# One change to a perceiver block: transposed inputs, and a first cross attention that goes by pairs of tiles

## The chip, the core and the metric

The kernel runs on one core of a Trainium2 chip. TensorE is called PE here, VectorE DVE, ScalarE ACT, GpSimd POOL, SyncE SP; SPq and ACTq are the DMA issues of SP and ACT. The metric is the device time of one execution in microseconds, and the median of the runs is what counts.

## The reference, cut to what matters

`x` is 32 x 64 x 128 (the latents), `ctx_1024` is 32 x 1601 x 128 (the context), both f32. Six layers follow one another, each added to `x`:

```python
x = x + L0_xattn(layernorm(x), ctx, ctx, mask, Wq, bq, Wk, bk, Wv, bv, Wo, bo)  # 16 heads of 8
x = x + L0_attn(layernorm(x), ...)           # a delta rule by chunks of 64
x = x + L0_ffn(layernorm(x), router, up, dn) # 8 experts, top 2
x = x + L1_xattn(ctx, layernorm(x), Wq, Wkv, Wout, gm, bm, gl, bl)
x = x + L1_attn(layernorm(x), ...)           # a gated delta rule, 4 heads
x = x + L1_ffn(layernorm(x), ...)            # attention over the batch, then 8 experts
# in L0_xattn, per batch and head:
#   softmax(q @ k.T * scale, masked keys out) @ v, then @ Wo.T + bo
# in L1_xattn (8 heads of 64): keys and values from concat(ln(ctx, gm, bm), ln(latents, gl, bl)) @ Wkv,
#   queries from ln(latents, gl, bl) @ Wq; softmax of q @ k.T / scale minus its maximum
```

`scale` is the head size to the power -1/2, so in L1_xattn the division by it makes scores large: both cross attentions need the row maximum before the exponential, and precise scores.

## The kernel before, in words

The stages run one after another: setup and **xattn0** (0 to 1098 us), **delta0**, **moe0**, **xattn1** (1426 to 2562 us), **delta1**, **ffn1** (from 2846 us). Each stage writes one instruction list per engine; semaphores alone order the engines, and each list is in a fixed, hand-written order. The latents stay on chip in `k.x` (16 tiles of 128 rows).

**xattn0** (`stage_xattn0`) takes one step per batch, 32 steps; steps 0 and 27 to 31 are written out, the others are in a loop of two. The 1601 keys are 13 tiles of 128 (the last has 65). What a step `b` does:

- *Scores* (`scores`, L794): for tile `j`, eight bf16 products of the stacked keys `KS` with the queries `QS` of all 16 heads, into the two-bank tensor `SC`. The keys are split in three bf16 pieces `KP[0..2]`, whose stack of 97 rows plus bias rows is multiplied in one go. ACT takes the exponential into `PT` (`probs`, L522).
- *Products* (`products`, L805, L809): `PT` times the values `V` in f32, 8 instructions. The row sums come from POOL's running sum `acc` (L444) of nine tiles, closed by `total` (L817), and for the other tiles from a product with ones (L809).
- *Maxima* for the next batch (`tops`, L771, L775): 26 units, each a bf16 product of the keys with the queries into one of the two banks `A`, and a reduction on DVE (L607, L610). `top` (L784) transposes the result `mxm` into `M`, and `topped` (L621, DVE) writes it as the rows of `QS` that subtract the maximum.
- *Context and keys* for later batches: four transposes `turn(b+3)` (L732) into the bank `M`, copied by ACT (`turned`, L486) to `CT`; `keys(b+2, c)` (L743) and `values(b+2, c)` (L759) for the four column chunks; then `keys` on ACT (first piece, L494), `residue` on DVE (L590), `second` on ACT, `third` on POOL (L433).
- *Transfers*, all on SP: `load(b+4)`, then two `spill`s of `KP` to memory (`KD`, L353; 12 issues), then two `stack`s of eight transfers each back into `KS` (L363), with the bias rows (L359).

At the front, the query weights are transposed, the layer norm of `x` and the queries are made, split into three pieces, written to memory (`QD`) and spread by heads into `QP` (L333, `spread`): batches 0 to 7 from SP, the others from ACT. The order there on SP is spill 0 (two halves), the pieces, stack 0 first half, spread, stack 0 second half, then batch 1.

**xattn1** (`stage_xattn1`) also has one step per batch, with 8 pairs of tiles `u`. The context is loaded again by rows into `C`, and its layer norm is made three batches ahead: `stats` and `moments` (DVE), `power` (POOL, L1639), `norm` (DVE, L1869, 13 tensor_scalar). `turn`/`turned` transposes it; `gain` (POOL, L1646, L1656) makes the value side. The maxima of the next batch are `tops` (L2036 on PE, L1875 on DVE), closed by `top` (L1884, L2047, L1888). At its start the stage loads ten weight tensors and transposes three (L1977), makes the products `GH` and `HH` (L1986, L1988), and only then transposes the norm (L220).

**Layer norm of the latents** (`norm_vector`, `norm_pool`, `norm_tensor`, `norm_scalar`): DVE takes 16 statistics (L188), 16 aggregates (L191), one addition (L194 or L196), POOL one power of 16 columns (L208), DVE 16 scalings (L201), PE 16 transposes (L220) in four chunks, ACT four copies. **ffn1** starts with four weight transposes (L2841 to L2844) ahead of them, and with two DVE copies that regroup weights (L2753, L2764).

The step of xattn0 on PE, which the change rewrites:

```python
for j in range(NK):
    us = units(j) if n1 else ()
    for u in us[0:1]: tops(b + 1, 1 - a, u)
    if j + 1 < NK: scores(b, a, j + 1)
    elif n1: scores(b + 1, 1 - a, 0)
    for u in us[1:2]: tops(b + 1, 1 - a, u)
    ...                       # keys, values, turn
    for u in us[2:]: tops(b + 1, 1 - a, u)
    products(b, a, j)
```

## Time and profile before

| | us |
|---|---|
| median of 3 runs | 3082.73 (3077.76 to 3084.12) |
| the profiled execution | 3079.37 |
| its span, and mean granted clock | 3077.6, 0.962 |
| PE busy | 2819.4 (92%), weight loads 1618.6 (53%) |
| DVE busy | 1978.6 (64%) |
| ACT busy | 1479.6 (48%) |
| POOL busy | 1906.0 (62%) |
| DMA | 233.18 MB, mean 76 GB/s |
| POOL sums L444 | 596.7 in 252 instructions of 2368 ns |
| ACT exponentials L522 | 425.8 in 416 |
| DVE maxima L607 | 506.4 in 768 of 685 ns |

Busy shares are means over stages of different make: PE is near 95% in both cross attentions and 60 to 80% at the stage starts. A timeline row gives start, duration, engine, line and operands, and in brackets the idle time before it with what ended it; a matmul row's end is modelled, so starts of neighbours are the safer measure.

### The profile page before, as it was taken

To read this page: it belongs to the slowest core of one execution; us is meant where nothing else is said; L and a number is where in the kernel's file an instruction comes from. 1 tells how busy PE (TensorE), PEld (TensorE's weight loads), DVE (VectorE), ACT (ScalarE), POOL (GpSimd) and SP (SyncE) were. 2 spreads that over 40 slices of the span, in tenths; PEclk is the share of its full clock that TensorE was granted. 3 is DMA by queue.
4 is the path that set the end of the run, shared out by engine and by line. 5 is a ranking of instruction groups with operands and counts; after the bars stand their busy time and mean duration, and the time that the engine had idled before them with its cause. 6 is when DMAs were issued, how large, how long until landed. Compare 5 with 4: busy or idle time off the path is not lost. (4 is left out here: it accounts for less than half of the span.)

```text
span 3077.6 us, 66754 instructions
## 1 busy us (share of the span) xinstructions
PE 2819.4 (92%) x22718; PEld 1618.6 (53%) x22765; DVE 1978.6 (64%) x4504; ACT 1479.6 (48%) x2385; POOL 1906.0 (62%) x1278
## 2 busy tenths in 40 slices
PE   5799999999999978998899999999999997888789
PEld 2355555555555566775344444444444443777356
DVE  5477777777777744114667767767767744776653
ACT  3466666666666522333544444444444434223633
POOL 5487878787878721001488888888888872553500
PEclk8899999999999989998999999999999998999789
DMA  7655555555555210001000000000000000000300
GB/s 184 187 174 193 177 190 181 184 186 179 194 175 188 100 58 1 1 0 39 22 33 21 21 32 21 21 32 21 21 32 21 21 1 9 3 3 2 85 5 10
DMA packets 146463, 233.18 MB, mean 76 GB/s; under 512 B 16787, under 2 KB 85851, under 8 KB 146076
## 3 DMA queue, kind: packets, MB, share of 16 engines
q1 hardware_dynamic: 145180, 228.87, 22.7%
q10 hardware_dynamic: 1152, 2.49, 0.6%
q8 instruction: 91, 1.49, 0.2%
q14 instruction: 40, 0.33, 0.0%
HBM read 147.80 MB, written 83.52 MB: 75 GB/s over the span
## 5 line engine op out<-in xcount | busy, mean ns | idle before, releaser
L444 POOL TENSOR_TENSOR sb_a_acc<-sb_a_acc,sb_a_PT 128x1024 f32<-128x1024 f32 x252 | 596.7, 2368 | 36.6 <-ACT sb_a_PT L522 30.3
L522 ACT ACTIVATE sb_a_PT<-ps_a_SC 128x1024 f32<-128x1024 f32 (+1 forms) x416 | 425.8, 1023 | 315.3 <-PE ps_a_SC L794 291.7
L607 DVE TENSOR_REDUCE sb_a_mx<-ps_a_A 128x1 f32<-128x512 f32 x768 | 506.4, 685 | 97.0 <-PE ps_a_A L771 91.8
L1686 POOL TENSOR_TENSOR sb_a_acc<-sb_a_acc,sb_a_PT 128x512 f32<-128x512 f32 (+2 forms) x384 | 487.5, 1269 | 37.3 <-ACT sb_a_PT L1782 10.9
L1782 ACT ACTIVATE sb_a_PT<-ps_a_SC 128x1024 f32<-128x1024 f32 (+2 forms) x256 | 234.3, 915 | 563.0 <-PE ps_a_SC L2061 329.3
L1875 DVE TENSOR_REDUCE sb_a_mx<-ps_a_A 128x1 f32<-128x512 f32 x384 | 256.5, 679 | 280.1 <-PE ps_a_A L2036 240.1
L2080 PE MATMUL ps_a_PV<-sb_a_PT,sb_a_XN 128*128 128x512 f32 (+2 forms) x896 | 434.3, 601 | 2.2 <-ACT sb_a_PT L1782 0.7
L2061 PE MATMUL ps_a_SC<-sb_a_QX,sb_a_XT 128*128 128x512 f32 (+1 forms) x832 | 396.7, 596 | 0.1
L771 PE MATMUL ps_a_A<-sb_a_KS,sb_a_QS 97*128 97x512 bf16 x768 | 301.9, 394 | 30.6 <-issue 17.7
L794 PE MATMUL ps_a_SC<-sb_a_QS,sb_a_KS 105*128 105x128 bf16 (+1 forms) x3328 | 257.3, 220 | 13.4 <-DVE sb_a_QS L621 13.4
L805 PE MATMUL ps_a_PV<-sb_a_PT,sb_a_V 128*32 128x256 f32 (+1 forms) x3328 | 266.7, 392 | 0.4 <-issue 0.3
L794 PEld LDWEIGHTS ps_a_SC<-sb_a_QS,sb_a_KS 105*128 105x128 bf16 (+1 forms) x3328 | 217.8, 99 | 83.8 <-ACT sb_a_PT L522 23.2
L2061 PEld LDWEIGHTS ps_a_SC<-sb_a_QX,sb_a_XT 128*128 128x128 f32 (+1 forms) x832 | 152.0, 186 | 202.3 <-issue 199.7
L2080 PEld LDWEIGHTS ps_a_PV<-sb_a_PT,sb_a_XN 128*128 128x128 f32 (+2 forms) x896 | 163.5, 191 | 131.3 <-issue 117.2
L208 POOL TENSOR_TENSOR sb_rstd<-sb_rstd,sb_half 128x16 f32<-128x16 f32 x8 | 23.3, 2907 | 291.9 <-DVE sb_rstd L194 240.9
L444 POOL TENSOR_TENSOR sb_a_acc<-sb_a_PT 128x1024 f32<-128x1024 f32 x32 | 75.4, 2357 | 199.7 <-ACT sb_a_PT L522 199.7
L1646 POOL TENSOR_TENSOR sb_a_XN<-sb_a_C,sb_a_gm 128x1536 f32<-128x1536 f32 x64 | 123.6, 1956 | 92.8 <-PE ps_a_PV L2080 92.1
L771 PEld LDWEIGHTS ps_a_A<-sb_a_KS,sb_a_QS 97*128 97x128 bf16 x768 | 74.5, 97 | 181.9 <-DVE sb_a_mx L607 106.2
L1869 DVE TENSOR_SCALAR sb_a_C<-sb_a_C,sb_a_cag,sb_a_crs 128x128 f32<-128x128 f32 (+1 forms) x416 | 170.0, 480 | 0.0
L1453 DVE SCALAR_TENSOR_TENSOR sb_x<-ps_a_D,sb_a_comb,sb_x 128x128 f32 x128 | 36.2, 344 | 180.7 <-PE ps_a_D L1407 180.5
L1431 ACT ACTIVATE sb_a_H<-ps_a_U 128x512 f32<-128x512 f32 x128 | 76.2, 597 | 139.4 <-PE ps_a_U L1398 139.3
L1656 POOL TENSOR_TENSOR sb_a_XN<-sb_a_XN,sb_a_bm 128x1536 f32<-128x1536 f32 x64 | 122.9, 1940 | 30.9 <-PE ps_a_PV L2017 23.1
(516 smaller groups left out, 5265.3 us busy)
## 6 DMA issues: line engine op xcount, KB each, us to landing
sb_a_C<-in_ctx_dram SPq DMA_DIRECT2D x64, 768.0 KB
a_KD<-sb_a_K SPq DMA_DIRECT2D x192, 256.0 KB, 4.1
sb_a_KS<-a_KD SPq DMA_DIRECT2D x256, 192.0 KB
a_KD<-sb_a_K SPq DMA_DIRECT2D x192, 144.2 KB, 2.7
sb_a_KS<-a_KD SPq DMA_DIRECT2D x256, 108.2 KB
sb_a_QP<-a_QD ACTq DMA_DIRECT2D x6, 384.0 KB, 14.7
sb_a_up<-in_moe_up_dram SPq DMA_DIRECT2D x1, 2048.0 KB, 7.9
sb_a_dn<-in_moe_dn_dram SPq DMA_DIRECT2D x1, 2048.0 KB, 12.0
```

Source lines behind the costliest of these rows:

```text
L444: pool.tensor_tensor(acc[:, :], first[:, :], PT[slot(a, j)][:, :], ALU.add).then_inc(s["acc"], 1)
L522: act.activation(PT[slot(a, j)][0:n, :], SC[(a + j) % 2][0:n, :], ACT.Exp).then_inc(s["exp"], 1)
L607: v.tensor_reduce(mx[:, p, c:c + 1], A[u % 2][:, :], AXX, ALU.max).then_inc(s["am"], 1)
L771: mm = pe.matmul(A[u % 2][:, :], QS[a][0:ROWM + 1, p, :], KS[a][0:ROWM + 1, p, 512 * c:512 * c + 512], start=True, stop=True)
L794: mm = pe.matmul(SC[(a + j) % 2][0:m, P * p:P * p + P], KS[a][0:ROWS, p, P * j:P * j + m], QS[a][0:ROWS, p, :], start=True, stop=True)
L805: mm = pe.matmul(PV[32 * g:32 * g + 32, 0, :], V[a][0:m, j, 32 * g:32 * g + 32], PT[slot(a, j)][0:m, G * T * g:G * T * g + G * T], start=( ...
L1686: pool.tensor_tensor(acc[a][0:m, :], first, PT[u % 4][0:m, HQ * i:HQ * i + HQ], ALU.add).then_inc(s["acc"], 1)
L1782: act.activation(PT[u % 4][0:m, 0:n], SC[u % 2][0:m, 0:n], ACT.Exp).then_inc(s["exp"], 1)
L1869: v.tensor_scalar(C[a][0:m, j, :], C[a][0:m, j, :], cag[a][0:m, j, 0:1], crs[a][0:m, j:j + 1], ALU.subtract, ALU.mult)\
L1875: v.tensor_reduce(mx[:, u % 4, u // 4:u // 4 + 1], A[u % 2][:, :], AXX, ALU.max).then_inc(s["am"], 1)
L2061: mm = pe.matmul(o, XT[a][:, col(j):col(j) + m], QX[a][:, :, :], start=True, stop=True)
L2080: mm = pe.matmul(PV[:, :], XN[a][0:m, j, :], PT[u % 4][0:m, HQ * i:HQ * i + HQ], start=(j == 0), stop=(j == NK))
```

## The change

The host prepares transposed copies: the context (`ctx_T`, by batch 128 x 1601), the weights of the first attention (`L0_xattn_WT`), those of xattn1 (`L1_xattn_WT`, `L1_xattn_cols`) and of ffn1 (`ffn1_w`). The transposes and copies of them leave the kernel; xattn1's weights are loaded in delta0 and ffn1's in delta1, into memory that stays allocated until then. In xattn0 a step goes by seven groups of two tiles; scores are two tiles ahead, products come in twos, `keys` and `residue` of half a batch are made a step earlier, POOL sums eight tiles, `top` uses a bank of `A`, and the closing work of a batch (`final`, `invert`) stands at the end of DVE's step. `load` comes behind spills and stacks. The layer norms of the latents go by four chunks. In xattn1, ACT applies the context's norm, and `moments` comes after the last maximum. Core of the diff:

```diff
-    COUNT = (0, 2, 2, 2, 2, 3, 3, 3, 3, 3, 3, 0, 0)
+    COUNT = (3, 5, 5, 5, 5, 3, 0)
+    SUMS = (1, 2, 4, 5, 6, 7, 8, 9)
 # SP
             def step(b, a, n2, n4):
-                if n4:
-                    load(b + 4, a)
                 if n2:
                     for g in range(2):
                         spill(b + 2, a, g)
                     for g in range(2):
                         stack(b + 2, a, g)
+                if n4:
+                    load(b + 4, a)
 ...
+            pieces(0)
+            sp.wait_ge(s["qw"], 48)
+            spread(sp, *SPANS[0], s["ldq0"])
             for g in range(2):
                 spill(0, 0, g)
-            pieces(0)
             stack(0, 0, 0)
-            sp.wait_ge(s["qw"], 48)
-            spread(sp, *SPANS[0], s["ldq0"])
-            stack(0, 0, 1)
             pieces(1)
             for g in range(2):
                 spill(1, 1, g)
+            stack(0, 0, 1)
+            load(2, 0)
+            for g in range(2):
                 stack(1, 1, g)
 # POOL
+                    if n2 and j in (1, 4, 7):
+                        third(b + 2, 1 + (1, 4, 7).index(j))
+                    if n3 and j == 9:
+                        third(b + 3, 0)
 # ACT
-            spread(act, *SPANS[1], s["ldq1"])
-            probs(0, 0, 0)
-            values(1, 1, 3)
-            step(0, 0, True, True, True)
+            step(0, 0, True, True, True)
+            spread(act, *SPANS[1], s["ldq1"])
 # PE, step of xattn0
+                for g in range(NG):
+                    us = list(units(g)) if n1 else []
+                    def maxima(n):
+                        for u in us[0:n]:
+                            tops(b + 1, 1 - a, u)
+                        del us[0:n]
+                    if g == 0 and n2:
+                        keys(b + 2, a, 2)
+                    if g + 1 < NG:
+                        for j in pair(g + 1):
+                            if g > 0:
+                                maxima(1)
+                            scores(b, a, j)
+                        maxima(1)
+                    if g == 1 and n2:
+                        keys(b + 2, a, 3)
+                    if g == 2 and n2:
+                        values(b + 2, a, 0)
+                    if g in (4, 5) and n3:
+                        keys(b + 3, 1 - a, g - 4)
+                    if g > 0:
+                        maxima(1)
+                    if g == NG - 1 and n1:
+                        top(b + 1)
+                    for j in pair(g):
+                        products(b, a, j)
+                    maxima(len(us))
+                    if g == 3 and n2:
+                        values(b + 2, a, 1)
+                    if g == 5 and n2:
+                        values(b + 2, a, 2)
                 total(b)
                 if n2:
                     values(b + 2, a, 3)
+                if n1:
+                    for j in pair(0):
+                        scores(b + 1, 1 - a, j)
 # layer norm of the latents, DVE (c is a chunk of four tiles)
+    moments(0)
+    moments(1)
+    scaled(0)
+    moments(2)
+    scaled(1)
+    moments(3)
+    scaled(2)
+    scaled(3)
 # xattn1, ACT in place of DVE
+            def normed(b, a, c):
+                wait(act, s["nb"], b + 1)
+                for j in range(4 * c, min(4 * c + 4, NK)):
+                    m = wcols(j)
+                    act.activation(C[a][0:m, j, :], C[a][0:m, j, :], ACT.Identity, bias=nb[a][0:m, j:j + 1], scale=crs[a][0:m, j:j + 1])\
+                       .then_inc(s["z"], 1)
 # xattn1, DVE, end of a step
                 if one:
-                    top(b + 1, 1 - a)
+                    top(b + 1)
                 if three:
-                    norm(b + 3, 1 - a)
+                    moments(b + 3, 1 - a)
+                if one:
+                    topped(b + 1, 1 - a)
```

## Rows read from the trace of the kernel before

**Rows 1.** Timeline of DVE, maxima row into queries once per step: start us, us
```profile
81.50 1.23 DVE L621 TENSOR_TENSOR sb_a_QS<-ps_a_M,sb_negdiag 32x1024 bf16<-32x1024 f32 x1 [0.67 <-PE ps_a_M L784]
135.20 1.23 DVE L621 TENSOR_TENSOR sb_a_QS<-ps_a_M,sb_negdiag 32x1024 bf16<-32x1024 f32 x1 [1.02 <-PE ps_a_M L784]
...
1009.60 1.23 DVE L621 TENSOR_TENSOR sb_a_QS<-ps_a_M,sb_negdiag 32x1024 bf16<-32x1024 f32 x1 [1.02 <-PE ps_a_M L784]
```

**Rows 2.** Busy by stretch; columns PE, PEld, DVE, ACT, POOL, clock, DMA, GB/s
```profile
84.00:1044.00 960.00, 915.89 (x9591) 513.83 (x9590) 700.83 (x1166) 622.81 (x897) 747.28 (x419) 0.99 0.55 183
```

**Rows 3.** Timeline of PE in two steady steps
```profile
570.72 0.64 PE L805 MATMUL ps_a_PV<-sb_a_PT,sb_a_V 128*32 128x256 f32 x8
571.17 0.61 PE L809 MATMUL ps_a_PV<-sb_a_PT,sb_ones 128*32 128x256 f32 x8
...
589.94 0.60 PE L732 MATMUL ps_a_M<-sb_ident,sb_a_C 128*128 128x128 f32 x4
590.38 0.38 PE L771 MATMUL ps_a_A<-sb_a_KS,sb_a_QS 97*128 97x512 bf16 x1
590.69 0.64 PE L805 MATMUL ps_a_PV<-sb_a_PT,sb_a_V 128*32 128x256 f32 x8
591.26 0.39 PE L771 MATMUL ps_a_A<-sb_a_KS,sb_a_QS 97*128 97x512 bf16 x1
591.49 0.61 PE L794 MATMUL ps_a_SC<-sb_a_QS,sb_a_KS 105*128 105x128 bf16 x8
```

**Rows 4.** Timeline of DVE, three maxima reductions in a row
```profile
591.69 2.01 DVE L607 TENSOR_REDUCE sb_a_mx<-ps_a_A 128x1 f32<-128x512 f32 x3 [0.20 <-PE ps_a_A L771]
```

**Rows 5.** Groups by line, POOL, 300 to 1000 us: busy us, mean ns
```profile
L444 POOL TENSOR_TENSOR sb_a_acc<-sb_a_acc,sb_a_PT 128x1024 f32<-128x1024 f32 x181 | 427.5, 2362 | 11.5 <-ACT sb_a_PT L522 7.9
L433 POOL TENSOR_TENSOR sb_a_K<-sb_a_RK,sb_a_K 128x512 bf16<-128x512 f32 x92 | 87.4, 949 | 0.0
```

**Rows 6.** DMA, 540 to 640 us in 40 slices
```profile
GB/s 148 148 142 177 293 322 270 322 142 59 53 147 151 149 146 138 231 309 375 240 286 23 74 123 147 152 148 142 154 293 345 271 320 134 59 55 147 150 148 146
```

**Rows 7.** Timeline of SP and ACT, DMA issues: start us, us spent issuing
```profile
45.66 2.82 SPq L333 DMA_DIRECT2D sb_a_QP<-a_QD  x6
74.89 19.01 SPq L363 DMA_DIRECT2D sb_a_KS<-a_KD  x8
...
70.44 2.98 ACTq L333 DMA_DIRECT2D sb_a_QP<-a_QD  x6
```

**Rows 8.** Tile of the spread queries: time from issue to landing
```profile
DMA to landing us min/median/max: 5.1/11.5/22.9
```

**Rows 9.** Timeline of PE, first maxima product of the kernel
```profile
62.37 1.01 PE L771 MATMUL ps_a_A<-sb_a_KS,sb_a_QS 97*128 97x512 bf16 x2 [7.52 <-DVE sb_a_QS L599]
```

**Rows 10.** Waits of PE, 82 to 300 us: in total, times, longest
```profile
PE ps_a_A L771 <- issue: 17.2, 1, 17.2
```

**Rows 11.** Timeline of DVE, second layer norm of ffn1
```profile
2944.08 3.18 DVE L188 BATCH_NORM_STATS2 sb_st<-sb_a_HP 128x6 f32<-128x128 f32 x16
...
2951.55 4.19 DVE L201 TENSOR_SCALAR sb_a_Y<-sb_a_HP,sb_mv,sb_rstd 128x128 f32<-128x128 f32 x16 [3.01 <-POOL sb_rstd L208]
```

**Rows 12.** Timeline of POOL, powers of 13 and of 16 columns
```profile
1926.08 2.44 POOL L1639 TENSOR_TENSOR sb_a_crs<-sb_a_crs,sb_half 128x13 f32<-128x13 f32 x1
...
2850.80 2.90 POOL L208 TENSOR_TENSOR sb_rstd<-sb_rstd,sb_half 128x16 f32<-128x16 f32 x1 [0.29 <-DVE sb_rstd L194]
```

**Rows 13.** Timeline of PE, start of xattn1
```profile
1435.81 1.12 PE L1977 MATMUL ps_a_M<-sb_ident,sb_a_Wq 128*128 128x128 f32 x4 [11.02 <-DMA sb_a_blc<-in_L_xattn_bl_dram]
```

**Rows 14.** Waits of PE, 1600 to 2400 us
```profile
PE ps_a_A L2047 <- DVE sb_a_mxm L1884: 17.2, 12, 1.4
```

**Rows 15.** Groups by line and form, ACT, one activation of 64 rows
```profile
L1772 ACT ACTIVATE sb_a_XN<-sb_hn 64x128 f32 x28 | 8.6, 306 | 0.3
```

**Rows 16.** Timeline of PE, start of ffn1
```profile
2858.21 0.45 PE L2841 MATMUL ps_a_L<-sb_ident,sb_a_Wqr 128*128 128x128 f32 x1 [13.30 <-DVE sb_a_Wpp L2753]
...
2866.04 2.04 PE L2853 MATMUL ps_a5m_U<-sb_hT,sb_a_WqT 128*128 128x512 f32 x2 [2.19 <-DVE sb_a_WkT L2764]
```

More of the change, by code:

```diff
@@ L221, in norm_tensor, with norm_scalar @@
         mm.then_inc(s["turned"], 1)
-def norm_scalar(k, act, s, banks):
-    for c in range(NT // 4):
+def norm_scalar(k, act, s, banks, chunks=range(NT // 4)):
+    for c in chunks:
         act.wait_ge(s["turned"], c + 1)
@@ L662, in step, with parts @@
                     expand(b + 2, a)
[L664 to L667 removed]
+                if old:
+                    final(b - 1)
+                    invert(b - 1)
+            moments, scaled = norm_parts(k, v, s["n"])
+            def parts(h):
+                lo, hi = SPANS[h]
                 q, q1, q2, q3 = (t[:, lo:hi] for t in (QT, Q1, Q2, Q3))
@@ L676, in _ @@
                 v.tensor_tensor(q3, q, q2, ALU.subtract).then_inc(s["q3"], 1)
+            v.memset(mx[:, :, 4:5], 0.1 * MASKED).then_inc(s["mz"], 1)
+            moments(0)
+            moments(1)
+            scaled(0)
+            scaled(1)
+            moments(2)
+            moments(3)
+            parts(0)
+            scaled(2)
+            for c in range(4):
+                residue(0, c)
+            scaled(3)
+            parts(1)
             for c in range(4):
@@ L865, in _ @@
                 values(1, 1, c)
-            for c in range(4):
-                turn(2, 0, c)
             pe.wait_ge(s["qc"], NT // 4)
@@ L873, in _ @@
             top(0)
-            scores(0, 0, 0)
+            for j in pair(0):
+                scores(0, 0, j)
             values(1, 1, 3)
+            for c in range(2):
+                keys(2, 0, c)
             step(0, 0, True, True, True)
@@ L1796, in step @@
                         probs(b + 1, 1 - a, 0)
+                    if two and isinstance(b, int) and b == 0:
+                        if u == 4:
+                            for c in range(4):
+                                normed(2, 0, c)
+                    elif two and u in (0, 1, 3, 5):
+                        normed(b + 2, a, (0, 1, 3, 5).index(u))
                     if two and u == 3:
@@ L1810, in _ @@
             heads_in(0)
+            for c in range(4):
+                normed(0, 0, c)
             turned_queries(0, 0)
@@ L1925, in step @@
                         moments(2, 0)
-                    if first and u == 3:
-                        norm(2, 0)
-                    if u == 4 and three:
-                        moments(b + 3, 1 - a)
                     if first and u == 4:
```

540 lines of the change are left out of this document (253 added, 287 removed).

## The prediction

> **What bounds the kernel now.** I read the busy table first (TensorE 92%, the others 48 to 64%), then the busy time of each engine by stretch: the first cross attention (xattn0) is 960 us with PE busy for 916 and a granted clock of 0.99 [rows 2]. The waits of PE come next. In the steady steps they name almost nothing, so what sets a step there is PE's own stream: its instructions, their changes of type, and small waits. To get the step I took one operation that comes once a batch, the maxima row (L621) on DVE: (1009.60 - 135.20) / 28 = 31.23 us. Between its first two, however, lie 53.70 us [rows 1], 22.5 us more than a step. The stage starts and layer norms were read last, from timelines, since there nothing else hides a wait. DVE's maxima reductions are the second limit: 26 a step, three back to back in 2.01 us, so 0.67 each [rows 4] or 17.4 us of DVE in a step, through two PSUM banks that PE can be only two products ahead of.
>
> **xattn0, a steady step.** (a) The four context transposes go: one is at 589.94 and what follows it starts at 590.38, 0.44 us [rows 3]; three such and a short one of 65 rows, taken as 0.25, are 1.6 us. (b) Pairing makes six to seven fewer changes between bf16 and f32 work. A bf16 product before f32 work costs 590.69 - 590.38 = 0.31 us, before bf16 work 591.49 - 591.26 = 0.23; products (f32) before bf16 work cost 591.26 - 590.69 = 0.57, before f32 work 571.17 - 570.72 = 0.45 [rows 3]. So 0.20 per pair of changes, 1.3 us. (c) Tile 3 is no longer summed on POOL, which adds a product with ones on PE: 0.45 to 0.61 us [rows 3], taken as 0.5. PE's stream is then 31.2 - 1.6 - 1.3 + 0.5 = 28.8 us, and its present small waits (some 0.8 us) would leave 28.0. But the work taken away stood between maxima products and gave DVE time. In a group of the new order five maxima stand with one score block between two of them (0.23 + 0.44, with a block taken at the pitch of four transposes: 0.67 us, DVE's own pace) and two with nothing between; reduction of the first bank must end before the third product. Laid out by hand with 0.67 us per reduction, PE waits 0.27 to 0.3 us in each of four groups, 0.7 in the first group, where three maxima and a residue meet, and 0.4 for the first exp: 2.4 us together. I take 30.35 us, 0.9 less than now. Bounds: nothing saved at all (31.23, or above where the rival on stacks comes in), and all of it (28.0). 27 of 31 steps count: -24, from +0 to -87.
> The other engines have room. POOL does eight sums of 2.36 and thirds of 0.95 on average [rows 5], 22.8 us a step; ACT loses 2 us of copies. On SP the load of a batch is moved behind spills and stacks; it isn't needed until half a step later.
>
> **xattn0, front.** Now the first half of the queries is spread only at 45.66, behind 12 spills and 8 stacks [rows 7], the landing takes up to 22.9 us [rows 8], and PE waits 7.52 us for it before 62.37 [rows 9]. The change sends it before the spills, without weight transposes and with the norm's first chunk ready earlier (below). The new end is the second half of stack 0, which is queued behind both spills of batch 1. I take the first maxima row at 69 instead of 81.5: -12.5, from -18 to -5.
> **Step 0.** The 22.5 us above hold one wait of 17.2 us for a stack [rows 10]. SP spent 19.01 us on issuing those eight stack transfers, from 74.89, while ACT had queued six spreads of 384 KB at 70.44 [rows 7]. The change issues the spreads after step 0. Step 0 then takes a normal 31 plus 2 to 3 of catching up, and step 1 pays: 3 us in ACT's stream for the issues and some 2 of stack delay. 33.5 + 35.5 = 69 against 53.7 + 31.2 = 84.9: -16, from -20 to +1.
> By the Trainium skill ("Trainium Kernel Development and Optimization", Key Constraints) transfers issued by SP, ACT and POOL run on the same 16 DMA engines and interleave, so a change of issuer or place takes none away. The rows agree that they collide (19.01 us for eight issues); if they do so as hard in step 1, this term is +1 and not -16, which is rival 3.
> Keys are half a step ahead from the start, and the last two steps have fewer terms: -2.
>
> **Layer norms in four chunks.** Before, DVE has all statistics from 2944.08, waits 3.01 us for POOL's power, and scales from 2951.55 for 4.19 us, so 11.7 us in all [rows 11]. Powers of 16 and 13 columns take 2.90 and 2.44 us [rows 12], 0.15 a column by the difference, so an estimated 1.1 to 1.3 us for four, under 1.1 us of the next chunk's statistics. The wait goes, three additions of 0.17 come: -2.5 at each place where the last scaled tile gates (moe0, delta1, ffn1's second); -2 in delta0, where a power for the key norm follows. -9.5 in all, from -12 (PE also starts earlier) to -3.
>
> **xattn1.** Start: PE idles 11.02 us for weights until 1435.81 and then transposes them [rows 13]; both go, since they come from on-chip memory filled in delta0. What is late next is the path of the context: its statistics on DVE, the power, and now 26 scalings on ACT, at 0.31 us for 64 rows [rows 15] and so 8 to 10 us. I take -8, from -12 to -2, and -4 in the first step, whose DVE is emptier. Steady: in 800 us PE waited 12 times for the maxima reduction, 17.2 us in all [rows 14], once in two steps of 33 us. The change puts the last maximum before the moments of b+3 and takes 13 scalings off DVE, so this wait goes: 0.7 us x 29 steps = -20. It is late next by little: the row of the next batch is ready some 0.5 to 1 us before its scores. ACT gains 4 to 5 us in a step where it is idle more than half. Bounds: 0 (another wait takes its place) and -36 (1.2 us a step, with the DVE shorter).
>
> **ffn1.** PE's first real work, the queries, starts at 2866.04; the transposes of weights before it started at 2858.21 after 13.30 us idle [rows 16]. Without weights to turn and to copy the norm's transposes come at about 2850 and the queries at 2857.8: -8.2, from -10 to -4.
>
> **Sum.** -24 - 12.5 - 16 - 2 - 9.5 - 32 - 8.2 = -104 (the statistics before delta0 included). The profiled execution took 3079.4 us, span 3077.6 plus 1.8 around it; that gives 2975. The median of the runs shown is 3.3 above the profiled one, so 2978.
>
> **Rivals.** 1. *DVE eats the steady step*: the period stays 31.2, because the 17.4 us of reductions set the pace of each group and PE's shorter stream only waits. For: the 0.67 above equals DVE's pace exactly. Against: DVE is busy 700.8 of 960 us [rows 2], 22.8 in a step. 2978 + 24 = 3002. 2. *All of PE's savings come through*: the waits overlap, the period is 28.6: -71 instead of -24, 2931. The stack loop below stands against it. 3. *The spread collision moves to step 1*: 2978 + 17 = 2995. 4. *xattn1 gains nothing*: the chain from moments to row, now later by the moments, or ACT's turned copies behind 13 scalings, takes the place of the wait; 2978 + 24 = 3002. 5. *Other side: the stack's landing becomes the loop.* In each step, after the previous exp, POOL must do six sums and three thirds (6 x 2.36 + 2 x 1.17 + 0.33 = 16.9, up to 18.6 with its waits), then the last spill (taken as 1.2, between nothing and the 4.1 of a large one's landing on the page) and the first stack land before the first maxima product 2.4 us into the next step. Eight stacks of 192 KB at 148 GB/s [rows 6] take 10.6 us, with start-up 11.8. Loop: 1.9 + 18.6 + 1.2 + 11.8 - 2.4 = 31.1 at the worst, 29.3 if POOL isn't held up: nearly no margin. With the load now right behind the stacks, landing may become 15 to 17 us; the period then is 34.5 to 36. From 34.1 on the whole is slower (80 us of other gains over 28 steps above 31.2); at 35.5 it is 2978 + 28 x 5.1 = 3122. Against: the load is behind the stacks in the queue, and rows 6 show 300 GB/s just before.
>
> **Chances.** Forecast 0.41 (its own range 2955 to 3000), rivals 1 to 5: 0.17, 0.15, 0.09, 0.10, 0.05; the rest, 0.03, is no change. Two of the small ones together give 3020. The range of 8 in 10 is 2918 to 3030: the low end is rival 2 with a better xattn1, the high end rival 1 with 3 or 4. Within 0.2% (6 us, about what a measurement of this kernel can tell) 0.03; faster 0.92; slower 0.05, which is rival 5.
>
> **What would show it.** Maxima rows of DVE 30.3 us apart, with waits of PE for L607's reductions of 2 to 3 us a step (rival 1: 31.2; rival 2: under 29; rival 5: the first maxima product of each step waiting for a DMA). First row at 69, second at 102, no wait of over 5 us for a stack in steps 0 and 1. No wait of PE for the maxima reduction in xattn1 and pairs of steps of 64.8 instead of 66.2 us. Queries of ffn1 at 12 us from its start instead of 20. The forecast is wrong if the steady step isn't within 0.6 us of 30.35, for that term alone moves it by 17.

## The result, and the profile after

The changed kernel takes 3050.39 us (median of 4 runs, 3047.61 to 3054.61) against 3082.72 before: a ratio of 0.9899, with a 95% interval of 0.9882 to 0.9916 (such pairs stand behind the times below too). It is 1% faster where 3.4% were forecast, and the time lies above the range of 2918 to 3030. Its profiled execution has a span of 3049.7 us (before 3077.6), a mean granted clock of 0.954 (before 0.962). First the busy line of the page:

```profile
PE 2776.7 (91%) x22530; PEld 1624.8 (53%) x22577; DVE 1832.9 (60%) x4139; ACT 1558.4 (51%) x2665; POOL 1851.6 (61%) x1303
```

PE is busy 43 us less than before, but the span is only 28 us shorter: PE now waits more. To see in which stage, the statistics that open each stage, in the timeline of DVE (start, duration), first of the kernel before, then of the changed one:

```profile
1098.54 3.19 DVE L188 BATCH_NORM_STATS2 sb_st<-sb_x 128x6 f32<-128x128 f32 x16 [0.55 <-PEq L335]
...
1182.99 3.19 DVE L188 BATCH_NORM_STATS2 sb_st<-sb_x 128x6 f32<-128x128 f32 x16 [0.32 <-PEq L1165]
...
1426.50 3.19 DVE L188 BATCH_NORM_STATS2 sb_st<-sb_x 128x6 f32<-128x128 f32 x16 [0.32 <-PEq L1479]
...
2562.51 3.19 DVE L188 BATCH_NORM_STATS2 sb_st<-sb_x 128x6 f32<-128x128 f32 x16 [0.33 <-PEq L1606]
...
2846.18 3.19 DVE L188 BATCH_NORM_STATS2 sb_st<-sb_x 128x6 f32<-128x128 f32 x16 [0.55 <-PEq L2210]
```

```profile
1109.10 0.87 DVE L189 BATCH_NORM_STATS2 sb_st<-sb_x 128x6 f32<-128x128 f32 x4 [0.55 <-PEq L359]
...
1195.62 0.87 DVE L189 BATCH_NORM_STATS2 sb_st<-sb_x 128x6 f32<-128x128 f32 x4 [0.32 <-PEq L1236]
...
1436.99 0.87 DVE L189 BATCH_NORM_STATS2 sb_st<-sb_x 128x6 f32<-128x128 f32 x4 [0.33 <-PEq L1555]
...
2542.72 0.87 DVE L189 BATCH_NORM_STATS2 sb_st<-sb_x 128x6 f32<-128x128 f32 x4 [0.33 <-PEq L1678]
...
2826.61 0.87 DVE L189 BATCH_NORM_STATS2 sb_st<-sb_x 128x6 f32<-128x128 f32 x4 [0.55 <-PEq L2276]
```

The stages from these starts (the last ends with the span), and xattn0 cut further at the maxima rows [rows 1], which are L661 in the changed kernel. Its rows 0, 1, 2 and 29 in the timeline of DVE:

```profile
76.55 1.23 DVE L661 TENSOR_TENSOR sb_a_QS<-ps_a_A,sb_negdiag 32x1024 bf16<-32x1024 f32 x1 [0.67 <-PE ps_a_A L829]
116.97 1.23 DVE L661 TENSOR_TENSOR sb_a_QS<-ps_a_A,sb_negdiag 32x1024 bf16<-32x1024 f32 x1 [1.20 <-PE ps_a_A L829]
170.12 1.23 DVE L661 TENSOR_TENSOR sb_a_QS<-ps_a_A,sb_negdiag 32x1024 bf16<-32x1024 f32 x1 [1.11 <-PE ps_a_A L829]
...
1015.82 1.23 DVE L661 TENSOR_TENSOR sb_a_QS<-ps_a_A,sb_negdiag 32x1024 bf16<-32x1024 f32 x1 [1.20 <-PE ps_a_A L829]
```

| stretch | before | after | change | forecast |
|---|---|---|---|---|
| xattn0 to maxima row 0 | 81.5 | 76.6 | -4.9 | -12.5 |
| rows 0 to 2 | 84.9 | 93.6 | +8.7 | -16 |
| rows 2 to 29 (27 steps) | 843.2 | 845.7 | +2.5 | -24 |
| row 29 to the end of xattn0 | 88.9 | 93.3 | +4.3 | -2 |
| delta0 | 84.5 | 86.5 | +2.1 | -2 |
| moe0 | 243.5 | 241.4 | -2.1 | -2.5 |
| xattn1 | 1136.0 | 1105.7 | -30.3 | -32 |
| delta1 | 283.7 | 283.9 | +0.2 | -2.5 |
| ffn1 | 231.4 | 223.1 | -8.3 | -10.7 |
| sum | | | -27.9 | -104 |

xattn1 came as forecast as a whole, and ffn1 within 2.4 us. The missing 65 us of the 76 are xattn0's: it is 10.6 us longer, where 54.5 less were forecast. Its steady step is 845.7 / 27 = 31.32 us in the mean, against 31.23. The mean hides two kinds of step. Before, each took 31.2 us; now 22 of the 27 take 29.5 to 31.9 at a clock of 1.00, and five take 33.6 to 34.8 at 0.90. One of the five, the step behind it, and a piece of the first (columns as in [rows 2]):

```profile
576.70:610.90 34.20, 31.13 (x319) 18.24 (x322) 23.54 (x39) 18.36 (x27) 22.73 (x13) 0.90 0.53 175
610.90:640.79 29.89, 28.16 (x319) 16.95 (x322) 23.29 (x40) 18.34 (x27) 22.73 (x13) 1.00 0.57 186
...
586.00:589.00 3.00, 2.64 (x16) 1.32 (x13) 1.98 (x3) 0.00 (x0) 1.46 (x1) 0.50 0.96 279
```

PE waited 1.83 us for a stack until 584.03, and from 584.5 to about 591 the clock was at 0.50. The same 319 instructions kept PE busy for 31.1 us instead of 28.2. The waits of PE in 600 us (in total, times, longest):

```profile
PE ps_a_A L819 <- DMA sb_a_KS<-a_KD: 25.3, 18, 2.5
PE ps_a_A L819 <- DVE sb_a_mx L647: 10.6, 20, 0.6
PE ps_a_SC L839 <- ACT sb_a_PT L537: 5.9, 20, 0.3
```

Some 19 steps: 1.3 us each for a stack, which the kernel before did not have there, and 0.9 us for reductions and exponentials (0.2 more for the short reductions, L823). The DMA queue of SP in one such step without the two bias rows (start, us spent issuing), POOL's last third of this step and of the next, the first maxima product of the next step, which waited, and the DMA rate from 608 to 672 us in 40 slices:

```profile
634.11 5.84 SPq L385 DMA_DIRECT2D sb_a_KS<-a_KD  x8
640.98 6.12 SPq L385 DMA_DIRECT2D sb_a_KS<-a_KD  x8
```

```profile
632.30 0.32 POOL L439 TENSOR_TENSOR sb_a_K<-sb_a_RK,sb_a_K 128x65 bf16<-128x65 f32 x1
...
663.12 0.31 POOL L439 TENSOR_TENSOR sb_a_K<-sb_a_RK,sb_a_K 128x65 bf16<-128x65 f32 x1
```

```profile
647.77 0.39 PE L819 MATMUL ps_a_A<-sb_a_KS,sb_a_QS 97*128 97x512 bf16 x1 [1.47 <-DMA sb_a_KS<-a_KD]
```

```profile
GB/s 152 151 150 149 143 155 211 265 337 400 378 313 252 126 40 25 78 45 154 152 151 149 146 148 137 185 260 306 389 382 365 230 190 108 5 92 29 133 152 151
```

Read them as one circle. POOL's last third ends at 632.6; the last spill and the bias row follow; the first stack is issued at 634.11, 1.5 us behind the third, the second stack right behind it at 640.98. The rate comes up to 150 GB/s only at about 637 and stays at 137 to 154 until 648. The first maxima product of the next step starts at 647.77, 13.7 us behind the issue and after 1.47 us of idleness. The next third ends 15.7 us later, so from one third to the next the circle takes 663.43 - 632.62 = 30.8 us. The second stack's rest, the load and the spills follow at up to 389 GB/s, until about 661, and then come some 3 us with little transfer, in which SP waits for the next third. Busy time of that stretch (columns as in [rows 2]):

```profile
640.00:646.00 6.00, 5.70 (x67) 3.87 (x68) 4.44 (x8) 3.76 (x7) 0.54 (x2) 1.00 0.40 149
```

At 149 GB/s the 16 DMA engines are busy for 0.40 of their time. Steps 0 and 1: PE's waits from 77 to 180 us, and the clock by stretch, first from maxima row 0 on:

```profile
PE ps_a_A L819 <- DMA sb_a_KS<-a_KD: 17.7, 3, 13.6
```

```profile
76.55:92.00 15.45, 10.31 (x38) 5.58 (x39) 2.81 (x4) 5.80 (x9) 4.61 (x3) 0.50 0.61 209
...
150.00:160.00 10.00, 3.49 (x22) 1.70 (x23) 1.13 (x2) 0.00 (x0) 0.00 (x0) 0.50 0.66 217
```

The wait of 17.2 us of [rows 10] is not gone, it has moved by one step, as one of 13.6 us: the last product before it starts at 140.12, the first behind it at 156.51, and PE then runs at 0.50, that is at 1.2 GHz, for some 5 us. Step 0 is no normal step either: its first 15 us ran at 0.50, as did the 16 us before it, in which PE is busy for half of the time (8.35 of 16.55 us).

### The profile page after: what moved, and what is told of

Same layout as the page of the kernel before. It is cut to its first block and busy times, and to the rows that moved or that the text cites. A ratio compares the mean times of both kernels' runs of the same rounds, so it can differ in the third digit from the quotient of the medians.

```text
span 3049.7 us, 66129 instructions
## 1 busy us (share of the span) xinstructions
PE 2776.7 (91%) x22530; PEld 1624.8 (53%) x22577; DVE 1832.9 (60%) x4139; ACT 1558.4 (51%) x2665; POOL 1851.6 (61%) x1303
## 5 line engine op out<-in xcount | busy, mean ns | idle before, releaser
L647 DVE TENSOR_REDUCE sb_a_mx<-ps_a_A 128x1 f32<-128x512 f32 x768 | 498.2, 687 | 178.6 <-PE ps_a_A L819 176.5
L537 ACT ACTIVATE sb_a_PT<-ps_a_SC 128x1024 f32<-128x1024 f32 (+1 forms) x416 | 410.0, 1025 | 285.8 <-PE ps_a_SC L839 278.5
L450 POOL TENSOR_TENSOR sb_a_acc<-sb_a_acc,sb_a_PT 128x1024 f32<-128x1024 f32 x221 | 523.2, 2367 | 48.5 <-ACT sb_a_PT L537 38.9
L1946 DVE TENSOR_REDUCE sb_a_mx<-ps_a_A 128x1 f32<-128x512 f32 x384 | 256.6, 679 | 293.1 <-PE ps_a_A L2099 233.0
L819 PE MATMUL ps_a_A<-sb_a_KS,sb_a_QS 97*128 97x512 bf16 x768 | 289.9, 405 | 93.4 <-DMA sb_a_KS<-a_KD 62.5
L850 PE MATMUL ps_a_PV<-sb_a_PT,sb_a_V 128*32 128x256 f32 (+1 forms) x3328 | 240.5, 395 | 1.6 <-issue 1.6
L229 POOL TENSOR_TENSOR sb_rstd<-sb_rstd,sb_half 128x4 f32<-128x4 f32 x32 | 32.4, 1020 | 297.6 <-DVE sb_rstd L196 241.5
L439 POOL TENSOR_TENSOR sb_a_K<-sb_a_RK,sb_a_K 128x512 bf16<-128x512 f32 (+1 forms) x128 | 121.4, 950 | 92.2 <-ACT sb_a_K L515 92.0
L1835 ACT ACTIVATE sb_a_C<-sb_a_C,sb_a_nb,sb_a_crs 128x128 f32<-128x128 f32 (+1 forms) x416 | 172.1, 483 | 0.4
L524 ACT ACTIVATE sb_a_V<-ps_a_M 128x512 f32<-128x512 f32 (+1 forms) x122 | 59.9, 491 | 178.0 <-PE ps_a_M L806 176.3
L1702 POOL TENSOR_TENSOR sb_a_crs<-sb_a_crs,sb_half 128x13 f32<-128x13 f32 x32 | 78.0, 2439 | 110.3 <-DVE sb_a_nb L1941 110.3
## 6 DMA issues: line engine op xcount, KB each, us to landing
sb_a_QP<-a_QD ACTq DMA_DIRECT2D x6, 384.0 KB, 19.9
```

The costliest lines, as they stand in the source:

```text
L450: pool.tensor_tensor(acc[:, :], first[:, :], PT[slot(a, j)][:, :], ALU.add).then_inc(s["acc"], 1)
L537: act.activation(PT[slot(a, j)][0:n, :], SC[(a + j) % 2][0:n, :], ACT.Exp).then_inc(s["exp"], 1)
L647: v.tensor_reduce(mx[:, p, c:c + 1], A[u % 2][:, :], AXX, ALU.max).then_inc(s["am"], 1)
L819: mm = pe.matmul(A[u % 2][:, :], QS[a][0:ROWM + 1, p, :], KS[a][0:ROWM + 1, p, 512 * c:512 * c + 512], start=True, stop=True)
L850: mm = pe.matmul(PV[32 * g:32 * g + 32, 0, :], V[a][0:m, j, 32 * g:32 * g + 32], PT[slot(a, j)][0:m, G * T * g:G * T * g + G * T], start=( ...
L1835: act.activation(C[a][0:m, j, :], C[a][0:m, j, :], ACT.Identity, bias=nb[a][0:m, j:j + 1], scale=crs[a][0:m, j:j + 1])\
```

## The experiments

All are timed beside the kernel before (3079.6 to 3081.8 us in these sets); unless said otherwise the edit is made in the changed kernel. The edits are shown shortened. A run alone has no interval; four runs of the changed kernel lie within 7 us.

**1. Is it the stack, and is it DVE?** Two theories of the step of 31.3 us: the loop through POOL, spill, stack and first product; or DVE's 17.4 us of reductions. The first edit (e1) lets the first stack go ahead of the last spill:

```diff
-                    for g in range(2): spill(b + 2, a, g)
-                    for g in range(2): stack(b + 2, a, g)
+                    spill(b + 2, a, 0)
+                    spill(b + 2, a, 1, (0, 1))   # pieces 1 and 2
+                    stack(b + 2, a, 0)
+                    spill(b + 2, a, 1, (2,))
+                    stack(b + 2, a, 1)
```

> SP's order in a step of xattn0: first spill, pieces 1 and 2 of the second spill, first stack, piece 3 of the second spill, second stack; all else as in the changed kernel. Stack theory (the step is set by the loop POOL thirds, last spill, first stack, first maxima product): the first stack is issued about 4.6 us earlier in a step, PE's waits for it (1.4 us a step) go, its clock dip at the end goes; the period falls from 31.3 to 29.9 (29.6 to 30.3), the whole by 35 to 45 us, to about 3010. DVE theory (26 reductions of 0.67 us set the step): the period stays within 0.2 us of 31.3 and the whole at 3050.

3069.56 us (ratio to before 0.9963, 0.9950 to 0.9976): 19 us slower than the changed kernel, so neither theory's number. SP's queue:

```profile
612.03 0.73 SPq L381 DMA_DIRECT2D sb_a_KS<-out_dram  x1
614.42 5.84 SPq L385 DMA_DIRECT2D sb_a_KS<-a_KD  x8
620.31 0.46 SPq L375 DMA_DIRECT2D a_KD<-sb_a_K  x1
628.34 5.84 SPq L385 DMA_DIRECT2D sb_a_KS<-a_KD  x8
```

The first stack is not issued 4.6 us earlier: it now waits for the landing of the first spill (bias row at 612.03, stack at 614.42). The single spill issued behind it at 620.31 landed only just before 628.34, 8 us later, and the second stack waits for that; that it stood behind the eight stacks on the same engines is the reading that fits. The order had made one queue out of writes and reads that wait for each other. The first maxima product shows one thing more:

```profile
628.22 0.39 PE L820 MATMUL ps_a_A<-sb_a_KS,sb_a_QS 97*128 97x512 bf16 x1 [1.24 <-DMA sb_a_KS<-a_KD]
```

The first stack took 628.22 - 614.42 = 13.8 us, as long as before, although the second was not yet issued. Steps of some 30 and some 34.5 us alternate here, 32.3 in the mean. So the loop through POOL was not all: the transfers of a step are also a chain of their own, 16 us of stacks at 150 GB/s (2.46 MB) and 10 to 12 us of load and spills, and in the changed kernel only the 3 us or so in which SP waits for POOL separate the two bounds.

The second (e4) takes half of the columns of DVE's large reductions:

```diff
-                    v.tensor_reduce(mx[:, p, c:c + 1], A[u % 2][:, :], AXX, ALU.max)
+                    v.tensor_reduce(mx[:, p, c:c + 1], A[u % 2][:, 0:256], AXX, ALU.max)
```

> The changed kernel whose 24 large maxima reductions a step in xattn0 read only 256 of 512 columns, so the maximum is taken over half of the keys (that part of the computation is left out). DVE theory: DVE loses some 24 x 0.27 = 6 us a step, and the period falls by 1 to 2 us, the whole by 30 to 60. Stack theory: PE arrives earlier at the first maxima product and waits longer there, the period stays at 31.0 to 31.4, the whole within 10 us of 3050.

3046.62 us in one run, 1 us under the fastest run of the changed kernel. PE's waits, the same 600 us:

```profile
PE ps_a_A L819 <- DMA sb_a_KS<-a_KD: 42.3, 19, 3.2
```

The waits for a stack grew from 25.3 to 42.3 us: PE only comes earlier to it. The DVE theory (rival 1) falls.

**2. Half of the bytes (e8).** The kernel leaves out the other half of each new stack.

```diff
+                mid = (lo + hi) // 2      # from batch 2 on
-                    sp.dma_start(KS[a][0:96, w, lo:hi], KD[a][:, 16 * w:16 * w + 16, lo:hi])
+                    sp.dma_start(KS[a][0:96, w, lo:mid], KD[a][:, 16 * w:16 * w + 16, lo:mid])
```

> The changed kernel with half of the columns in every stack transfer of xattn0 from batch 2 on (the other half of the keys on chip stays that of an older batch, so that part of the computation is left out). Transfer theory (stacks at 150 GB/s, 16 us of a step, in series with spills and load, make the step): 8 us of transfers go, PE's wait for a stack goes, the period of the maxima rows falls from 31.3 to 29.5 to 29.9 and the whole by 40 to 50 us beside 3050, with PE's waits for DVE's reductions left. DVE theory: the period stays at 31.0 or more and the whole above 3040.

2985.81 us in one run, and maxima rows 88.48 / 3 = 29.49 us apart:

```profile
603.32 1.23 DVE L663 TENSOR_TENSOR sb_a_QS<-ps_a_A,sb_negdiag 32x1024 bf16<-32x1024 f32 x1 [1.11 <-PE ps_a_A L831]
...
691.80 1.23 DVE L663 TENSOR_TENSOR sb_a_QS<-ps_a_A,sb_negdiag 32x1024 bf16<-32x1024 f32 x1 [1.12 <-PE ps_a_A L831]
```

So the stacks' transfer time makes the step, and without it the step is 0.9 us shorter than forecast, not equal to it. Part of the gain is the clock, which is at 1.00 in all of these steps.

**3. What makes a stack slow?** Longer rows first (e10, and e11 with the spread of experiment 6): one transfer of 1601 columns for two of 1024 and 577.

```diff
-                for w in range(NP): sp.dma_start(KS[a][0:96, w, lo:hi], ...)   # for g = 0, 1
+                for g in range(2): sp.wait_ge(s[f"kw{g}"], 96 * b + 96)
+                for w in range(NP):
+                    sp.dma_start(KS[a][0:96, w, 0:S], KD[a][:, 16 * w:16 * w + 16, 0:S])
```

> Each batch's stack goes as 8 transfers of 1601 columns, not 16 of 1024 and 577, at the front too. It starts only behind the last score tile of the older batch, 3 us later than now, but has half the rows to move. Per-row theory (a stack is slow because each row of 1.1 to 2 KB costs the same time, some 0.2 us per transfer engine): the whole stack lands 10 to 11 us after its start and not 16, the wait before the first maxima product goes, the period is 29.9 to 30.6, the whole 3010 to 3035. Per-byte theory (150 GB/s whatever the row length): it lands 16 us later, the first maxima product waits 4 to 6 us in each step, the period is 34 to 36 and the whole is 3130 to 3190.

> e10's merged stacks and the spread of the queries by steps together. Per-row theory: both gains add, as the transfers then have room for one spread a step: 2990 to 3015. Per-byte theory: 3110 to 3175, 15 to 20 under e10.

3456.40 us (1.1219, 1.1200 to 1.1238), and 3432.77 (1.1155, 1.1128 to 1.1181) with the spread by steps: the per-byte side, and e10 375 us over the kernel before where it said 50 to 110. SP's queue, PE's waits, and the DMA rate from 635 to 680 us in 40 slices:

```profile
635.31 5.89 SPq L385 DMA_DIRECT2D sb_a_KS<-a_KD  x8
...
679.58 6.15 SPq L385 DMA_DIRECT2D sb_a_KS<-a_KD  x8
```

```profile
PE ps_a_A L816 <- DMA sb_a_KS<-a_KD: 161.6, 13, 13.5
```

```profile
GB/s 23 20 94 154 154 157 154 154 211 265 222 343 400 385 387 180 154 171 137 150 147 142 129 7 0 0 221 173 0 0 130 132 0 0 101 31 0 0 0 0
```

679.58 - 635.31 = 44.3 us from one stack to the next: with one group the stack starts only behind the last score of the older batch, nothing overlaps, and PE idles over 12 us a step. The rate in the stack is 154 to 157 GB/s with rows of 1601 columns, against about 150 with 1024. The row's length is not it.

Then the shape. A stack transfer reads 6 pieces of 16 rows, and 0.40 of 16 engines is 6.4. The Trainium skill ("DMA: Bandwidth & Descriptors", Why a DMA increments its semaphore by 16 and not by 1) says that a transfer issued by SP runs on the largest number of engines, up to 16, that divides the slowest dimension of both sides: 6 and 96 give 6. The first try puts 16 rows outermost (e12; e14 is the same edit in the kernel before, e13 adds both edits of experiment 6):

```diff
-                for w in range(NP):
-                    sp.dma_start(KS[a][0:96, w, lo:hi], KD[a][:, 16 * w:16 * w + 16, lo:hi])
+                for r in range(len(PIECES)):
+                    sp.dma_start(KS[a][16 * r:16 * r + 16, :, lo:hi],
+                                 KD[a][r][:, lo:hi].rearrange("(w i) s -> i w s", i=16))
```

> The changed kernel with each stack of xattn0 as 6 transfers, one per piece, whose slowest dimension is the 16 rows of a piece, not as 8 whose slowest dimension is the 6 pieces; the same bytes to the same places. Engine-count theory (the 8 transfers use 6 of the 16 DMA engines: busy share 0.40, 150 GB/s): the rate in a stack rises to 300 GB/s or more, a stack lands in 6 to 8 us, PE no longer waits for one in the steady step, the period falls from 31.3 to 29.5 as with half the bytes, the wait in step 1 shrinks below 5 us, and the whole is 2975 to 2995. Rival (150 GB/s is a limit of reading this memory): rate, period and the whole stay (3045 to 3055).

> The kernel before with that one edit alone. If PE's stream sets its steady step, as the prediction said, the period stays at 31.0 to 31.3, only the 17.2 us wait of step 0 shrinks to under 5 and the wait for the queries may change: the whole 3055 to 3070. If its steady step was bound by transfers too, the period falls below 30.8 and the whole below 3050.

> e12 with the spread of the queries by steps (as e2) and stack 0's second half issued before the spills of batch 1 (as e3). Engine-count theory: the first maxima row at 70 us, rows 1 and 2 at 31 us distances, period 29.5: 2960 to 2980, under e12 by 5 to 15. Rival: 3025 to 3035, since only e2's and e3's gains are left.

e12 takes 3124.86 us (1.0152, 1.0135 to 1.0169), e14 3115.28 (1.0115, 1.0099 to 1.0132) and e13 3110.14 (1.0101, 1.0084 to 1.0118): all slower than the kernel before. Of e12, the DMA rate in 600 to 664 us, and the queue's share of 16 engines:

```profile
GB/s 184 128 118 120 127 129 122 109 128 138 120 164 176 384 380 375 351 245 2 96 156 122 118 119 123 119 117 119 111 128 122 125 155 264 391 374 371 340 133 0
q1 hardware_dynamic: 7104, 11.37, 97.1%
```

All 16 engines are busy now (97.1%), and move 109 to 138 GB/s in a stack: in each transfer they write into the same 16 partitions. That this is what holds them is the reading that fits the next kernel; it wasn't tried by itself. The count of engines had changed as expected, the rate had not. So the second try (e15) keeps 96 partitions as the target and makes the source's slowest dimension 96 too, by the layout of the keys in memory:

```diff
-    KD = [... (len(PIECES), P, S) ...]
+    KD = [... (NP, len(PIECES), 16, S) ...]
-                            sp.dma_start(KD[a][r][:, lo:hi], KP[n][:, lo:hi])
+                            sp.dma_start(KD[a][:, r, :, lo:hi], KP[n][:, lo:hi])
-                    sp.dma_start(KS[a][0:96, w, lo:hi], KD[a][:, 16 * w:16 * w + 16, lo:hi])
+                    sp.dma_start(KS[a][0:96, w, lo:hi], KD[a][w].rearrange("r i s -> (r i) s")[:, lo:hi])
```

> The changed kernel with another layout of the keys in memory: the 96 rows (piece, row) of one stack transfer lie behind each other, so the transfer's slowest dimension is 96 on both sides and its target still spans 96 partitions. The bytes and the order are as in the changed kernel; the spills now have a slowest dimension of 8. Engine-count theory (6 engines at 25 GB/s each made the 150 GB/s; by-piece stacks were slow since 16 engines wrote to 16 partitions): stacks move at 280 GB/s or more, spills at about 200, the first maxima product waits for none, the period is 29.5 to 30.0, the whole 2985 to 3010. Rival (a limit of reading what was just written, whatever the shape): stacks stay at 150, spills get slower, the period is 32 or more, the whole above 3070.

2982.65 us (0.9681, 0.9664 to 0.9697), 68 us under the changed kernel and 2 under the range expected. Busy time of a stretch of spills, one of stacks, and of four whole steps (columns as above), and the maxima rows at the ends of these steps:

```profile
612.00:618.00 6.00, 5.76 (x64) 3.80 (x62) 4.95 (x9) 3.75 (x6) 5.92 (x4) 1.00 0.53 179
628.00:634.00 6.00, 6.00 (x77) 3.83 (x69) 4.75 (x9) 3.03 (x6) 0.58 (x2) 1.00 1.06 274
600.06:717.99 117.93, 112.37 (x1264) 68.00 (x1267) 92.95 (x157) 73.43 (x105) 90.83 (x52) 1.00 0.66 196
```

```profile
600.06 1.23 DVE L661 TENSOR_TENSOR sb_a_QS<-ps_a_A,sb_negdiag 32x1024 bf16<-32x1024 f32 x1 [1.12 <-PE ps_a_A L829]
...
717.99 1.23 DVE L661 TENSOR_TENSOR sb_a_QS<-ps_a_A,sb_negdiag 32x1024 bf16<-32x1024 f32 x1 [1.12 <-PE ps_a_A L829]
```

PE's waits from 300 to 900 us:

```profile
PE ps_a_A L819 <- DVE sb_a_mx L647: 10.2, 20, 0.5
```

Stacks move at 274 GB/s with a share of 1.06, against 149 with 0.40; the spills, whose slowest dimension is now 8, at 179 with 0.53 instead of 300 to 400. The shares go as 16, 6 and 8 engines would. This also speaks against the rival that the new layout merely makes reading easier: by these counts an engine moves 274 / 16 = 17 GB/s now and moved 149 / 6 = 25 before, so each is slower, and the gain is in their number.

The step is 117.93 / 4 = 29.48 us, at a clock of 1.00 throughout, and has no wait for a transfer. The 27 steps give 50 us of the 68, step 1 gives 17 (36.3 us instead of 53.2), and the front loses 4: row 0 comes at 80.60, after 9.3 us of waiting for a stack. This is the forecast's 2975 to 2978 within 8 us, though not by its own terms.

**4. Was the kernel before bound by it as well?** The same layout there (e17):

> The same layout in the kernel before. If PE's own stream set its step, as the prediction said, the period stays at 31.0 to 31.3, and only step 0's wait of 17.2 us shrinks: 3060 to 3075. If transfers bound it already, the period falls below 30.8, the whole below 3055.

3073.36 us (0.9975, 0.9965 to 0.9985); maxima rows 62.48 / 2 = 31.24 us apart:

```profile
627.71 1.23 DVE L621 TENSOR_TENSOR sb_a_QS<-ps_a_M,sb_negdiag 32x1024 bf16<-32x1024 f32 x1 [1.02 <-PE ps_a_M L784]
...
690.19 1.23 DVE L621 TENSOR_TENSOR sb_a_QS<-ps_a_M,sb_negdiag 32x1024 bf16<-32x1024 f32 x1 [1.02 <-PE ps_a_M L784]
```

The layout is worth 7.5 us before the change, 5.5 of them in step 0 and 2.0 in the front, and 68 behind it. What the prediction said of the kernel before was right: PE's stream, with its small waits, set its step. How far under it the transfers lay no run says.

**5. What do the reductions cost, once the transfers are out of the way?** e15 with the reductions of e4 (e18):

> e15 with the large maxima reductions over 256 of 512 columns (the other half left out of the maximum). With the transfers out of the way this shows DVE's share: the hand schedule of the prediction put 2.4 us of waits for reductions in a step; if so the period falls by 1.5 to 2.4 us against e15 and the whole by 40 to 65. If it falls by under 0.8 us, PE's own stream sets the step.

2951.50 us in one run, rows 85.15 / 3 = 28.38 us apart:

```profile
613.54 1.23 DVE L661 TENSOR_TENSOR sb_a_QS<-ps_a_A,sb_negdiag 32x1024 bf16<-32x1024 f32 x1 [1.13 <-PE ps_a_A L829]
...
698.69 1.23 DVE L661 TENSOR_TENSOR sb_a_QS<-ps_a_A,sb_negdiag 32x1024 bf16<-32x1024 f32 x1 [1.18 <-PE ps_a_A L829]
```

1.1 us a step for DVE's other half, between the two bounds of the expectation, so less than the 1.5 that the hand schedule needs. In e15 PE waits 10.2 us in 20.4 steps for the long reductions, 0.5 a step, and the four steps above hold 117.93 - 112.37 = 5.6 us of idleness of PE, 1.4 a step, beside 28.1 of busy time.

**6. The collision and the front.** The spread one transfer a step (e2):

```diff
-            spread(act, *SPANS[1], s["ldq1"])
+            for b in range(1, 7):
+                step(b, b % 2, True, True, True, part=b - 1)  # one of the six behind probs(b, a, 9)
-                if not (isinstance(b, int) and b <= 2):       # expand, DVE
+                if not (isinstance(b, int) and b <= 7):
```

> The six transfers that spread the queries of batches 8 to 31 are issued one in each of steps 1 to 6 (steps written out on ACT and DVE), not all behind step 0, and DVE waits for them only from batch 8 on. Collision theory: the 13.6 us wait for a stack in step 1 and the clock of 0.5 behind it go, maxima rows 1 and 2 come 31 to 33 us apart and not 53.2, the whole is 20 us shorter (3028 to 3034). If the wait in step 1 has another cause (the batch-1 transfers queued late on SP), it stays over 8 us and the whole at 3045 or more.

3036.81 us (0.9853, 0.9836 to 0.9869), 13.6 under the changed kernel; maxima rows 1 and 2:

```profile
117.75 1.23 DVE L666 TENSOR_TENSOR sb_a_QS<-ps_a_A,sb_negdiag 32x1024 bf16<-32x1024 f32 x1 [1.20 <-PE ps_a_A L837]
...
148.01 1.23 DVE L666 TENSOR_TENSOR sb_a_QS<-ps_a_A,sb_negdiag 32x1024 bf16<-32x1024 f32 x1 [1.20 <-PE ps_a_A L837]
```

The long wait is gone (30.3 us from row 1 to row 2, not 53.2), but of the 22.1 us that row 2 is ahead of the changed kernel, 18.7 are left at row 7 and 14.9 at row 29. The five further steps with an added transfer thus cost 3.4 us; the 3.8 lost behind them, where both kernels issue the same, no run explains. At the front (e3):

```diff
             stack(0, 0, 0)
+            stack(0, 0, 1)
             pieces(1)
             for g in range(2):
                 spill(1, 1, g)
-            stack(0, 0, 1)
```

> At the front the second half of stack 0 is issued before the pieces and spills of batch 1, as before the change. Queue-order theory: the wait of 5.94 us before maxima product 17 of batch 0 goes and the first maxima row comes at 70 to 71 us instead of 76.6; batch 1's stacks come later and take part of it back in step 0, so the whole is 0 to 6 us shorter. Rival: the transfers are bandwidth-bound, and the row stays at 75 or later.

3043.39 us in one run, 4 under the fastest of the changed kernel's. Maxima row 0 comes at 71.52, 5.0 us earlier and half a microsecond past the expected 70 to 71.

All three together, e15's layout, e2 and e3 (e16):

> e15 with the spread of the queries by steps (e2) and stack 0's second half ahead of batch 1's spills (e3). Engine-count theory: first maxima row at 69 to 71 us, the next two 31 to 33 us apart, period 29.5 to 30.0: 2960 to 2985. Rival: as e15, less 15 to 20.

2966.40 us (0.9625, 0.9609 to 0.9641), the fastest of the runs that leave nothing out, 84 us under the changed kernel. Row 0 comes at 72.31 (69 to 71 expected), the steps 1 to 6 take 29.3 to 29.4 us, with an added transfer in each. Step 0, however, takes 40.7, where 31 to 33 were expected: like the 40.4 of the changed kernel and the 40.9 of e15. None of the edits shortens it; its first 15 us run at 0.50 in all three kernels.

**7. xattn1.** The context's norm back on DVE (`norm(b + 3)` behind `topped`, `moments` at pair 4; e7):

> xattn1 of the changed kernel with the context's norm back on DVE (13 scalings behind the maxima row) and its moments back at pair 4; weights, layer norm by chunks and the start as in the changed kernel. If the -30 us of xattn1 are the steady step's (moving the scalings and moments), the stage is 18 to 22 us longer than in the changed kernel, the waits for the maxima reduction (17 us in 800) are back, and the whole is 3068 to 3072. If they are the start's, the stage is under 8 us longer, the whole under 3058.

3073.53 us (0.9977, 0.9967 to 0.9987), 23 over the changed kernel. The stage takes 1127.2 us against 1105.7, and PE's waits for the maxima reduction from 1600 to 2400 us are back (17.0 us in 12 times, as in [rows 14]; none of that size in the changed kernel).

The 21.4 us are not the steady step's alone, for the edit also puts the first scalings, ahead of the first step, back on DVE. The rows in which DVE subtracts the maximum (one per batch) cut the stage:

| xattn1 | before | after | e7 |
|---|---|---|---|
| start to row 0 | 60.5 | 57.8 | 49.9 |
| row 0 to row 1 | 41.1 | 36.9 | 41.1 |
| row 1 to row 31 (30 steps) | 994.9 | 971.4 | 996.5 |
| row 31 to the end | 39.6 | 39.6 | 39.6 |

The steady steps gave 23.4 of the 30.3 us, the first step 4.2, and the start 2.7. With the scalings on DVE the start would have gained 10.5; on ACT they took 7.9 of that back.

## Why the prediction was wrong, point by point

- **The steady step of xattn0 (-24, measured +2.5).** The step that failed is the use made of the stack loop. Rival 5 worked it out as 29.3 to 31.1 us, "nearly no margin", and the sum then went on with 30.35 as if a bound of 31.1 were free. With its upper end the term is -3.5. The loop measured 30.8 us in the step read above, so 31.1 was nearly right, but by two errors: POOL's part, from the first maxima product to the last third, was taken as 1.9 + 18.6 - 2.4 = 18.1 us and took 15.7; the landing, taken as 11.8, took 13.7. The rate was as assumed (149 for 148 GB/s, 10.6 us for eight stacks); what was too small is the start-up, 1.2 us, for which the prediction shows no row, where 3.1 were left here. The second stack is not the reason, for e1 shows 13.8 us without it. The 22 steps at a clock of 1.00 take 30.7 us in the mean; the rest of the 31.32 is in the five steps at 0.90, and the prediction had no term for the clock. Experiment 2 shows the bound, e15 what it hides. Rival 5's own price, 3122, was for a landing of 15 to 17 us.
- **PE's own step (28.0 + 2.4 = 30.35).** With free transfers it is 29.48: in e15 28.1 us busy and 1.4 idle. The stream of 28.0 was right, and the term of 2.4 was mis-sized by 1 us. Rival 2 (28.6) was too low; rival 1 (31.2) named the right number for a wrong reason, as half the reductions show.
- **Step 0 and 1 (-16, measured +8.7).** Rival 3, given 0.09, is what happened, and more. Step 0 took 40.4 us where 33.5 were forecast: its first 15 us ran at a clock of 0.50, and PE was busy 34.1 us, with somewhat fewer instructions than a steady step has in 28.2. The prediction had no term for that, and e16 shows it too. Step 1 took 53.2 where 35.5 were forecast, with 13.6 us for one stack. I had priced the collision as "3 us in ACT's stream and some 2 of stack delay", without the six transfers' 2.3 MB: at the 150 to 300 GB/s of [rows 6] these alone are 8 to 16 us of transfers. The Trainium skill's rule cited there ("Trainium Kernel Development and Optimization", Key Constraints) spoke against the term, and the trace agrees with it, by the same 13.6 us.
- **The front (-12.5, measured -4.9).** The queries did come early; as said there, the second half of stack 0 became last. PE waited 5.9 us for it, and moving it ahead gave 5.0 us. Before that PE had waited 3.95 us for the first half, until 51.73.
- **The end of xattn0 (-2, measured +4.3).** It was not foreseen that a short wait can cost by the clock. PE waited 2.0 us for a stack until 1052.83, after 0.67 and 0.30 us for exponentials, and the clock stayed at 0.50 until about 1062. It begins (columns as above):

```profile
1053.00:1056.00 3.00, 3.00 (x19) 0.73 (x18) 0.83 (x2) 0.00 (x0) 2.08 (x1) 0.50 0.43 147
```

- **Layer norms.** moe0 -2.1, near the -2.5 forecast, ffn1's second -2.2 (from 11.7 to 9.4 us). delta0 was to gain 2 and lost 2.1: its norm ends only 0.6 us earlier, DVE's product behind it waits 1.3 us for POOL, and the projections run at a lower clock. In the 14 us from 1121 on it is 0.53, where it was 0.72 in the 12 us from 1111 on before. Why the clock was lower there no run tells. delta1's +0.2 was not followed up either.
- **xattn1 and ffn1.** -30.3 against -32, by errors that nearly cancel: steady -23.4 against -20, the first step -4.2 against -4, the start -2.7 against -8. That the steady part is the scalings' and moments' new place e7 confirms; at the start the scalings on ACT cost more than was left for them. ffn1's queries start 14.2 us into the stage instead of 19.9, 5.7 us earlier and not 8.2: the last tiles of the norm are turned from 2837.07 on only, and the queries then wait 1.3 us for ACT's copy of them.
- **The form of the forecast.** 0.92 for faster was right. Rivals 3 and 5 were given 0.14 together, although both rested on one resource that the text found nearly full; they came together, and their sum (2978 + 17 + 26) is 3021, of the measured 3050. The chance of 0.92 was for the sign alone.
